# GpSimd waits for landings inside its runs of indirect fetches, in the first sorted mixture of a long graph-network kernel

## The chip, the cores and the metric

The kernel runs on one core of one Trainium2 chip, as one launch. The metric is the device time of one execution in microseconds, the median over runs. Five engines run their own instruction streams beside each other: TensorE (PE), VectorE (DVE), ScalarE (ACT), GpSimd (POOL) and SyncE (SP); they meet only at semaphores and at barriers between blocks.

## The reference

Four graph layers and four feed-forward layers stand in turn, each added to the running x, each fed a layer norm of it. x is 128 graphs of 40 nodes of 128 features, so 5120 rows or 40 tiles of 128 rows. The change lies in the second feed-forward layer (`_L1_ffn_ref`), a mixture of 8 experts of which each row uses its best two:

```python
xn = (x - mu) * rsqrt(var + EPS) * gamma + beta
logits = einsum('bsd,de->bse', xn, Wr) + br
top_vals, top_idx = top_k(logits, 2)
w = softmax(top_vals, axis=-1)
w_full = einsum('bsk,bske->bse', w, one_hot(top_idx, 8))
for e in range(8):
    h = gelu(einsum('bsd,dh->bsh', xn, W1[e]) + b1[e])      # 128 -> 256
    y = y + (einsum('bsh,hd->bsd', h, W2[e]) + b2[e]) * w_full[..., e, None]
x = x + y
```

The third feed-forward layer routes by the result of an attention over a graph of 524288 random edges. Its edges are counted per pair of nodes, and that count is computed ahead, inside the mixture above: it needs nothing of the mixture.

## The kernel before, in words

`sparse_router` (from L1153) sorts the row numbers by expert. Each expert's list is padded to whole tiles of 256 rows (SL, two halves of 128, SLH = 2). There are 47 such tiles (NT). `sparse_moe` (L1671) then runs five streams in one block.

**GpSimd** issues all indirect DMAs, one instruction for 128 rows of 128 floats (64 KB). First 94 fetches (L1710), two for each tile, bring the normalised rows of a tile into one of six buffers `xg` (NX); from the seventh tile on a tile's pair waits until PE has turned the tile six before (`x_ps`). Then it waits until all results are stored in memory (`y_st`), and 80 return fetches (L1724) bring each row's two expert results back. They come in 8 parts (PARTS) of 5 row tiles (CT) with two fetches each. Part n lands on semaphore `c_in[n % 6]`, 16 counts for each fetch. From part 6 on a part first waits for DVE to have used the buffer (`added`).

**PE** turns a tile (L1734), multiplies it by W1 (L1743) and by W2 (L1751), two tiles ahead of the last step. **ACT** moves the turned tile (L1781), applies gelu (L1789) and copies the tile's expert weights into one of three buffers (L1796), which waits for an earlier result. **DVE** adds the bias (L1816), and between tiles does its share of the edge count: `nearest` (L2560: 32 maxima and 32 replacements, L2569) before the first tile, `search` after each. **SP** stores the results (L1855).

After the tiles DVE finishes the search and then works through the 8 parts of the return: for each part 5 or 6 steps `one_hot` (L2604, L2605: bf16 comparisons, 44 in all; PE multiplies each, L2690), then the wait for the part's ten fetches, and then ten multiply-adds into x (L1842). The block ends with DVE's last part; the layer norm of the next block (L351) needs all of it.

The same pattern without the edge count stands in the last layer (`sorted_moe`, results at L1625), and a third run of indirect fetches in `edge_router` (L2988, L2993; DVE's products at L2947). Neither is changed.

The functions that the change touches, as they are before it:

Of the kernel before, what the change touches and what calls it, by code (L numbers as in the profile page):

```python
# [953 lines left out]
SLH = SL // 128  # L954
# [716 lines left out]
def sparse_moe(nc, g, ex, out=None, count=None):  # L1671
# [2 lines left out]
    NX, NY, NW = 6, 4, 3  # L1674
    CT = 5
    PARTS, NC_ = TT // CT, 6
    name = ex.name
    with nc.cleanup_on_exit(), ExitStack() as ctx:
        sb = lambda s, shape: ctx.enter_context(nc.sbuf_tensor(f"{name}_{s}", shape, F32))
# [12 lines left out]
        x_in = [sem(f"x_in{i}") for i in range(NX)]  # L1692
        y_st = [sem(f"y_st{i}") for i in range(NY)]
        c_in = [sem(f"c_in{i}") for i in range(NC_)]
# [4 lines left out]
        @block.gpsimd  # L1699
        def _(pool):  # L1700
            pool.wait_ge(ex.stored, 32)
            if count is not None:
                count.prepare(pool)

            def gather(i):
                if i >= NX:
                    pool.wait_ge(x_ps, i - NX + 1)
                for h in range(SLH):
                    n = SLH * i + h
                    pool.indirect_dma_start(out=xg[:, i % NX, h, :], out_offset=None, in_=ex.xn_dram,  # L1710
                                            in_offset=bass.IndirectOffsetOnAxis(ap=ex.gidx[:, n:n + 1], axis=0)).then_inc(x_in[i % NX], 16)

            for i in range(NT):
                gather(i)
            for b in range(NY):
                pool.wait_ge(y_st[b], stores(b))
            for n in range(PARTS):
                if n >= NC_:
                    pool.wait_ge(added, n - NC_ + 1)
                for t in range(CT):  # L1720
                    if n > 0 and t == CT // 2:
                        pool.wait_ge(c_in[(n - 1) % NC_], 32 * CT * ((n - 1) // NC_ + 1))
                    for c in range(2):
                        pool.indirect_dma_start(out=yc[:, n % NC_, t, c, :], out_offset=None, in_=ex.y_dram,  # L1724
                                                in_offset=bass.IndirectOffsetOnAxis(ap=ex.pidx[:, n * CT + t, c:c + 1], axis=0)).then_inc(c_in[n % NC_], 16)
# [2249 lines left out]
def graph_network(nc, g):  # L3975

    with ExitStack() as ctx:
# [32 lines left out]
        with nc.sbuf_tensor("raw1", [128, TT, D], F32) as raw:  # L4010
            with nc.cleanup_on_exit(), ExitStack() as held:
                affine = (g.L1_ffn_gamma, g.L1_ffn_beta)
                ex = SparseExperts(nc, held, raw[:], g, "f1", 8, g.L1_ffn_W1, g.L1_ffn_b1, g.L1_ffn_W2, g.L1_ffn_b2, True, affine)
                with ExitStack() as early:
                    logits = RawLogits(nc, early, "f1l", 8, g.L1_ffn_Wr, g.L1_ffn_br, ex, affine)
                    raw_norm(nc, g, "n3", logits, twice=True)
                    sparse_router(nc, g, ex, logits)
                sparse_moe(nc, g, ex, count=EdgeCount(nc, held, g, keys, kept.keys_in))
            l2_gnn(nc, g, adjacency, search, tok=raw[:])
# [69 lines left out]
```

## Time and profile before

| | us |
|---|---|
| three runs, median (lowest to highest) | 3129.7 (3127.84 to 3139.87) |
| span of the profiled execution | 3331.1 |
| PE, DVE, ACT, POOL busy in that span | 2524.9, 2094.1, 1309.8, 721.2 |
| first fetch of L1710 to last one | 1658.67 to 1798.62 |
| first return fetch of L1724 to last one | 1823.15 to 1949.29 |
| start of DVE's last group of L1842 | 1993.44 |

The page gives the profiled execution's span and no other time of it; the runs are executions without the profiler. Times of rows are microseconds from the span's start, lengths of single instructions in the groups are ns. "Idle before <-releaser" names what the engine's wait ended with, inferred from semaphore events; "issue" is time in which it waited for nothing that the profile shows. Where a named releaser had long been done, it was another.

### The profile page before, as it was taken

The numbers are of one execution on the slowest core, as the hardware profiler recorded it, in microseconds if no ns is written. First come the engines' busy times: TensorE is split into PE (matmuls) and PEld (weight loads), VectorE is DVE, ScalarE is ACT, GpSimd is POOL, SyncE is SP. The second block draws the span as 40 slices with busy tenths as digits, with TensorE's granted clock in tenths as the row PEclk, the third lists the DMA queues.
The fourth block names the chain that finished last, engine by engine and source line by source line (L and its number), as shares of the span: only waits on it lengthen the run. The fifth ranks groups of instructions, "written<-read, shape, count | busy, mean of one in ns | idle before, by whom it ended". The sixth has DMA issues, their size and how long they took to land. (4 is left out here: it accounts for less than half of the span.)

```text
span 3331.1 us, 50319 instructions
## 1 busy us (share of the span) xinstructions
PE 2524.9 (76%) x18840; PEld 1620.7 (49%) x18840; DVE 2094.1 (63%) x4114; ACT 1309.8 (39%) x2407; POOL 721.2 (22%) x756
## 2 busy tenths in 40 slices
PE   6477999999999999965566178587649989971542
PEld 5334555555555555545255167344326666641542
DVE  6737787778788878856646397654743547761212
ACT  4333444444444444424555004232224444451431
POOL 0000000000000000010064630166610033306244
PEclk7688999999999999987689557698879978885766
DMA  4431112222221121113223101000012221111333
GB/s 76 130 107 42 49 49 49 55 60 53 50 49 49 49 49 49 46 40 121 67 77 75 43 17 18 13 5 5 5 32 70 52 50 41 41 33 56 94 87 93
DMA packets 189058, 178.78 MB, mean 54 GB/s; under 512 B 83700, under 2 KB 162177, under 8 KB 185977
## 3 DMA queue, kind: packets, MB, share of 16 engines
q1 hardware_dynamic: 168064, 137.00, 16.5%
q0 software_dynamic: 20768, 38.75, 4.8%
q8 instruction: 145, 2.38, 0.3%
q14 instruction: 81, 0.66, 0.1%
HBM read 139.11 MB, written 43.64 MB: 55 GB/s over the span
## 5 line engine op out<-in xcount | busy, mean ns | idle before, releaser
L3557 PE MATMUL hy_ps<-hy_uT,hy_win 128*128 128x512 f32 x1152 | 499.3, 594 | 0.0
L3557 PEld LDWEIGHTS hy_ps<-hy_uT,hy_win 128*128 128x128 f32 x1152 | 217.9, 190 | 283.0 <-issue 272.2
L2469 POOL DMA_DIRECT2D ek_w<-ek_src x32 | 17.8, 556 | 1162.6 <-DVE ek_dst L2491 1162.6
L3619 PE MATMUL hy_ps<-hy_wo,hy_yg 128*128 128x512 f32 x512 | 239.6, 613 | 14.5 <-ACT XNP L3762 8.7
L3055 PE MATMUL er_c<-XNG 128*128 128x400 f32 x480 | 184.0, 540 | 0.0
L3619 PEld LDWEIGHTS hy_ps<-hy_wo,hy_yg 128*128 128x128 f32 x512 | 94.2, 193 | 125.6 <-issue 99.3
L2690 PE MATMUL f_px<-XNG 128*128 128x40 bf16 x736 | 69.0, 266 | 98.2 <-DVE XNG L2605 66.0
L3841 DVE TENSOR_TENSOR_SCAN XNG<-XNG,hy_fx 128x2048 f32<-128x2048 f32 x32 | 141.6, 4425 | 3.0 <-issue 0.4
L2988 POOL DMA_INDIRECT er_gone<-er_nodes,er_sidx x120 | 123.7, 1031 | 36.6 <-issue 36.3
L3055 PEld LDWEIGHTS er_c<-XNG 128*128 128x128 f32 x480 | 97.6, 209 | 69.5 <-issue 14.5
L946 DVE TENSOR_TENSOR f_hg<-f_hs,f_gb 128x640 f32<-128x640 f32 x64 | 52.7, 825 | 109.9 <-ACT f_hs L928 91.3
L1625 DVE TENSOR_TENSOR f_ysl<-f_py,f_cur 128x256 f32<-128x256 f32 x54 | 22.9, 424 | 147.3 <-remote 69.4
L2690 PEld LDWEIGHTS f_px<-XNG 128*128 128x128 bf16 x736 | 60.6, 152 | 106.7 <-DVE XNG L2605 74.8
L3692 ACT ACTIVATE hy_swT<-hy_ps 64x160 f32<-64x160 f32 x256 | 76.2, 298 | 83.3 <-PE hy_ps L3524 78.3
L1567 PE MATMUL f_ph<-f_xT,f_cur 128*128 128x256 f32 x216 | 62.2, 414 | 59.6 <-DVE f_xT L1619 35.2
L1548 POOL DMA_INDIRECT XNP<-f_ys,f_pidx x80 | 78.2, 977 | 131.9 <-DMA f_ys<-f_ysl 108.2
L2279 PEld LDWEIGHTS g_ps<-ident,g_P 40*40 40x40 f32 x2048 | 84.3, 129 | 43.6 <-issue 34.1
L2947 DVE TENSOR_TENSOR XNG<-er_VW,er_MD 128x400 f32<-128x400 f32 x112 | 58.4, 573 | 73.4 <-DMA f_y<-f_ysl 54.7
L2252 PE MATMUL g_ps<-g_Z,g_wc 128*128 128x320 f32 x256 | 101.5, 542 | 1.1 <-ACT g_Z L2301 1.1
L1710 POOL DMA_INDIRECT f_xg<-f_xn,f_gidx x94 | 90.3, 961 | 51.0 <-issue 22.9
L1724 POOL DMA_INDIRECT XNP<-f_y,f_pidx x80 | 87.7, 1096 | 63.0 <-issue 23.8
L3792 DVE TENSOR_TENSOR hy_sw<-hy_ps,hy_blg 128x512 f32<-128x512 f32 x64 | 44.3, 692 | 90.7 <-PE hy_ps L3508 90.7
(698 smaller groups left out, 6123.4 us busy)
## 6 DMA issues: line engine op xcount, KB each, us to landing
XNG<-hy_decays SPq DMA_DIRECT2D x32, 1024.0 KB
hy_rb<-hy_inverse SPq DMA_DIRECT2D x128, 128.0 KB, 3.5
f_gb<-gate_rows SPq DMA_DIRECT2D x16, 640.0 KB, 5.1
g_KB<-g_keys SPq DMA_DIRECT2D x32, 320.0 KB
f_xg<-f_rows SPq DMA_DIRECT2D x54, 128.0 KB
f_ys<-f_ysl SPq DMA_DIRECT2D x54, 128.0 KB
f_y<-f_ysl SPq DMA_DIRECT2D x47, 128.0 KB
f_rows<-in_x_dram POOLq DMA_DIRECT2D x2, 2560.0 KB, 16.0
```

The costliest lines, as they stand in the source:

```text
L1548: pool.indirect_dma_start(out=yc[:, n % NC_, t, c, :], out_offset=None, in_=ex.y_dram[n // (PARTS // ex.HALVES)], in_offset=bass.IndirectO ...
L1710: pool.indirect_dma_start(out=xg[:, i % NX, h, :], out_offset=None, in_=ex.xn_dram, in_offset=bass.IndirectOffsetOnAxis(ap=ex.gidx[:, n:n ...
L1724: pool.indirect_dma_start(out=yc[:, n % NC_, t, c, :], out_offset=None, in_=ex.y_dram, in_offset=bass.IndirectOffsetOnAxis(ap=ex.pidx[:, n ...
L2252: mm = pe.matmul(psy, wc[:, h, :], Z[:, c % 2, h].rearrange("p b n -> p (b n)"), start=(h == 0), stop=(h == HD - 1))
L2279: mm = pe.matmul(pst[n % 2][j][rows(j), h, :], P[rows(j), c % 2, h, q, :], g.ident[rows(j), rows(j)], start=True, stop=True)
L2690: mm = pe.matmul(self.ph, self.OL[:, b, :, k], self.OH[:, b, :, k], start=False, stop=False, skip_group_check=True)
L2988: pool.indirect_dma_start(out=gone[:, par, u, :], out_offset=None, in_=tab_dram, in_offset=bass.IndirectOffsetOnAxis(ap=sidx[:, par, u:u + ...
L3055: mm = pe.matmul(flat(acc[j][:]), OD[:, 1 - par, u, j * 128:(j + 1) * 128], flat(X[:, u]), start=False, stop=False, skip_group_check=True)
L3557: mm = pe.matmul(p[:], win[:, t, m * 128:(m + 1) * 128], uT[:, t, :], start=(t == 0), stop=(t == KT - 1))
L3619: mm = pe.matmul(PS[4 + q % 2][:], yg[:, t, q * 128:(q + 1) * 128], wo[:, t, :], start=(t == 0), stop=(t == KT - 1))
L3692: ins = act.activation(o, p[:, :, j, 0:N], ACT.Copy)
L3841: dve.tensor_tensor_scan(L[:, a][:, st], dAb[:, a][:, st], E[:, st], 0.0, ALU.mult, ALU.add)
```

## The change

In `gather(i)` (tiles) GpSimd now waits, before the pair of tile 2 and before that of tile 4, until both fetches of the tile just before have landed. In the return it waits before row tiles 2 and 4 of each part until that part's earlier fetches have landed, and before row tile 0 of parts 1 to 7 until the part before has landed whole. The wait that stood before row tile 2 of parts 1 to 7, for the part before, goes.

```diff
+    BURST = 4
...
             def gather(i):
                 if i >= NX:
                     pool.wait_ge(x_ps, i - NX + 1)
+                elif i > 0 and SLH * i % BURST == 0:
+                    pool.wait_ge(x_in[i - 1], 16 * SLH)
                 for h in range(SLH):
...
                 for t in range(CT):
-                    if n > 0 and t == CT // 2:
+                    if t > 0 and t % (BURST // 2) == 0:
+                        pool.wait_ge(c_in[n % NC_], 32 * (CT * (n // NC_) + t))
+                    elif t == 0 and n > 0:
                         pool.wait_ge(c_in[(n - 1) % NC_], 32 * CT * ((n - 1) // NC_ + 1))
                     for c in range(2):
                         pool.indirect_dma_start(out=yc[:, n % NC_, t, c, :], out_offset=None, in_=ex.y_dram,
```

GpSimd's own order in the tile fetches of the kernel before; an xN stands for N like instructions, and the semaphore names are those of a semaphore's first user (n1_root is `x_ps` here):

```order
L2555 MEMSET ec_zero 128x128
L1710 DMA f_xg<-f_xn,f_gidx 128x128 x12
L1710 DMA f_xg<-f_xn,f_gidx 128x128 [waits n1_root]
L1710 DMA f_xg<-f_xn,f_gidx 128x128
L1710 DMA f_xg<-f_xn,f_gidx 128x128 [waits n1_root]
```

and the same place of the changed kernel (its line numbers are up to 5 higher; hy_ip_ps and hy_dt_half are `x_in[1]` and `x_in[3]`):

```order
L2560 MEMSET ec_zero 128x128
L1713 DMA f_xg<-f_xn,f_gidx 128x128 x4
L1713 DMA f_xg<-f_xn,f_gidx 128x128 [waits hy_ip_ps]
L1713 DMA f_xg<-f_xn,f_gidx 128x128 x3
L1713 DMA f_xg<-f_xn,f_gidx 128x128 [waits hy_dt_half]
L1713 DMA f_xg<-f_xn,f_gidx 128x128 x3
L1713 DMA f_xg<-f_xn,f_gidx 128x128 [waits n1_root]
```

The first twelve fetches are now three groups of four; the rest stands as it did.

The start of GpSimd's return fetches before (the four names at the head are the stores' `y_st`, hy_da_rdy is `c_in[0]`, hy_da_ld `c_in[1]`):

```order
L1724 DMA XNP<-f_y,f_pidx 128x128 [waits hy_dt_rdy,hy_da_exp,hy_dtln,hy_xs]
L1724 DMA XNP<-f_y,f_pidx 128x128 x13
L1724 DMA XNP<-f_y,f_pidx 128x128 [waits hy_da_rdy]
L1724 DMA XNP<-f_y,f_pidx 128x128 x9
L1724 DMA XNP<-f_y,f_pidx 128x128 [waits hy_da_ld]
```

and after the change:

```order
L1729 DMA XNP<-f_y,f_pidx 128x128 [waits hy_dt_rdy,hy_da_exp,hy_dtln,hy_xs]
L1729 DMA XNP<-f_y,f_pidx 128x128 x3
L1729 DMA XNP<-f_y,f_pidx 128x128 [waits hy_da_rdy]
L1729 DMA XNP<-f_y,f_pidx 128x128 x3
L1729 DMA XNP<-f_y,f_pidx 128x128 [waits hy_da_rdy]
L1729 DMA XNP<-f_y,f_pidx 128x128
L1729 DMA XNP<-f_y,f_pidx 128x128 [waits hy_da_rdy]
L1729 DMA XNP<-f_y,f_pidx 128x128 x3
L1729 DMA XNP<-f_y,f_pidx 128x128 [waits hy_da_ld]
```

Where a wait stood behind 14 fetches and then behind every 10, a part of ten is now cut into 4, 4 and 2, and each cut asks for the fetch just sent. On the other engines nothing moves.

## Rows read from the trace of the kernel before

**Rows 1.** Waits of the whole span, three: us in total, times, longest
```profile
DVE f_ysl L1625 <- remote: 69.4, 3, 29.0
...
DVE XNG L2604 <- DMA hy_xn<-XNP: 55.1, 2, 41.1
...
DVE XNG L2947 <- DMA f_y<-f_ysl: 54.7, 5, 11.6
```

**Rows 2.** Table of stretches of this block: length, busy times, clock, DMA
```profile
core 0: us, PE busy (x) PEld busy (x) DVE busy (x) ACT busy (x) POOL busy (x), PEclk, DMA share, GB/s
1666.50:1687.50 21.00, 6.41 (x33) 4.96 (x31) 7.65 (x48) 4.07 (x7) 13.50 (x15) 0.66 0.17 47
...
1847.00:1903.00 56.00, 2.73 (x32) 2.35 (x29) 1.63 (x2) 0.00 (x0) 39.75 (x42) 0.50 0.19 49
1903.00:1996.00 93.00, 64.58 (x689) 56.73 (x689) 89.15 (x166) 0.00 (x0) 29.55 (x20) 0.50 0.06 15
```

**Rows 3.** Instructions in order, return fetches of POOL beside DVE
```profile
1823.15 0.95 POOL L1724 DMA_INDIRECT XNP<-f_y,f_pidx  x1 [23.59 <-DMA f_y<-f_ysl]
...
1860.67 1.22 DVE L2604 TENSOR_TENSOR XNG<-XNG 128x2048 bf16<-128x2048 bf16 x1 [14.01 <-DMA hy_xn<-XNP]
...
1898.29 0.95 POOL L1724 DMA_INDIRECT XNP<-f_y,f_pidx  x1 [0.30 <-issue]
...
1903.37 1.23 DVE L2604 TENSOR_TENSOR XNG<-XNG 128x2048 bf16<-128x2048 bf16 x1 [41.08 <-DMA hy_xn<-XNP]
```

**Rows 4.** Waits of 1657 to 1830 us, this block's tile stage
```profile
DVE work L2569 <- issue: 13.3, 21, 1.3
...
ACT f_xT L1781 <- remote: 12.9, 2, 12.3
```

**Rows 5.** Instructions in order, first tile fetches and who uses them
```profile
1660.05 0.98 POOL L1710 DMA_INDIRECT f_xg<-f_xn,f_gidx  x1 [0.30 <-issue]
...
1662.60 0.95 POOL L1710 DMA_INDIRECT f_xg<-f_xn,f_gidx  x1 [0.30 <-issue]
1662.61 0.69 PE L1734 MATMUL f_px<-ident,f_xg 128*128 128x128 f32 x2 [10.12 <-DMA f_xg<-f_xn,f_gidx]
...
1665.12 0.95 POOL L1710 DMA_INDIRECT f_xg<-f_xn,f_gidx  x1 [0.30 <-issue]
1665.16 0.69 PE L1734 MATMUL f_px<-ident,f_xg 128*128 128x128 f32 x2 [1.86 <-DMA f_xg<-f_xn,f_gidx]
...
1667.72 0.69 PE L1734 MATMUL f_px<-ident,f_xg 128*128 128x128 f32 x2 [0.16 <-issue]
...
1693.33 0.38 PE L1734 MATMUL f_px<-ident,f_xg 128*128 128x128 f32 x2
...
1693.98 0.95 POOL L1710 DMA_INDIRECT f_xg<-f_xn,f_gidx  x1 [4.08 <-PE f_px L1734]
```

**Rows 6.** POOL's return fetches as groups: 1914.8 to 1950.3, then 1823 to 1846.6
```profile
L1724 POOL DMA_INDIRECT XNP<-f_y,f_pidx x20 | 29.5, 1477 | 21.4 <-DVE raw L1842 15.7 <-issue 5.8
...
L1724 POOL DMA_INDIRECT XNP<-f_y,f_pidx x19 | 18.4, 971 | 29.1 <-DMA f_y<-f_ysl 23.6 <-issue 5.5
```

**Rows 7.** Instructions in order, DVE in the return stage
```profile
1916.09 1.22 DVE L2604 TENSOR_TENSOR XNG<-XNG 128x2048 bf16<-128x2048 bf16 x1
...
1919.31 1.22 DVE L2604 TENSOR_TENSOR XNG<-XNG 128x2048 bf16<-128x2048 bf16 x1
...
1924.08 2.88 DVE L1842 SCALAR_TENSOR_TENSOR raw<-XNP,f_gates,raw 128x128 f32<-128x128 f32 x10
...
1926.87 1.22 DVE L2604 TENSOR_TENSOR XNG<-XNG 128x2048 bf16<-128x2048 bf16 x1
...
1993.44 2.87 DVE L1842 SCALAR_TENSOR_TENSOR raw<-XNP,f_gates,raw 128x128 f32<-128x128 f32 x10
```

**Rows 8.** Instructions in order, DVE results once the last tile fetch is sent
```profile
1805.63 0.42 DVE L1816 TENSOR_TENSOR f_ysl<-f_py,f_cur 128x256 f32<-128x256 f32 x1 [0.17 <-PE f_py L1751]
...
1807.60 0.42 DVE L1816 TENSOR_TENSOR f_ysl<-f_py,f_cur 128x256 f32<-128x256 f32 x1 [0.23 <-PE f_py L1751]
```

## The prediction, made before the changed kernel was run

> **What bounds the block now.** I read the block of the change in this order: the table of stretches, the instructions in order for POOL and DVE, the waits, and the groups of POOL's fetches. The reader is to see first that in the profiled execution the block has two holes. From 1666.5 to 1687.5 PE is busy for 6.41 us of 21 and DVE for 7.65, while POOL sends 15 fetches; from 1847 to 1903 DVE is busy for 1.63 us of 56 and POOL sends 42 [rows 2]. In the second hole DVE waits 14.01 and then 41.08 us before a one-hot step, under the name of a DMA of a layer long finished, and goes on 4 us after the last fetch of an unbroken run of 60 was issued (1898.29 + 0.95, against 1903.37) [rows 3]. In the first, ACT waits 12.3 us for a releaser the trace cannot name, and DVE loses 13.3 us in 21 gaps between replacements that wait for nothing [rows 4]. The DMA engines are only 17 to 19% busy there [rows 2], so it is no lack of transfer capacity.
>
> The question that decides the forecast is whether those holes are in the runs as well. The profiled span is 3331.1 us, the median run 3129.7: 201 us more. The same kind of wait, with a releaser that is none, stands in every other block in which POOL sends long runs of fetches: 69.4 us at L1625, 55.1 at L2604, 54.7 at L2947 [rows 1], 179 us in all; with the 13.3 us of rows 4 it is 193. That is nearly the whole difference, and I see no other place in the page for 200 us. I take it that the holes belong to the profiled execution and that the runs have next to none of them. Beside this stands a rule of the Trainium skill (NOTIFIC — the notification-queue block, "Overflow: three behaviours, one of which stalls the engine"): the block that writes the profiler's records holds its producers back rather than lose a record inside. No row here shows such a hold as such. A second rule (SBUF — State Buffer, "SBUF: two separate sides") says that PE and ACT never wait on another engine's port; the trace agrees in so far as the holes stop ACT as well, so a port is not what they are made of.
>
> **The block without the holes.** Two chains then race to the end of the return stage.
>
> DVE: from 1860.67 − 14.01 = 1846.7 [rows 3], where it is done with the search, 44 one-hot steps and 8 groups of adds. Two steps take 1919.31 − 1916.09 = 3.22, so 1.61 each; a group of adds 1926.87 − 1924.08 = 2.79 [rows 7]. 44 × 1.61 + 8 × 2.79 = 93.2 us, which ends at 1939.9.
>
> POOL: its fetches follow each other at 0.971 + 0.30 = 1.27 us where DVE does little, and at 1.477 + 0.30 = 1.77 where DVE is busy without a break [rows 6]: a DVE-busy microsecond costs POOL 0.50 / 1.77 = 0.28. From 1823.15 [rows 3], 80 × 1.27 = 101.6 and 0.28 × 93.2 = 26.3 give 1951.1; 1.6 for the last landing and 2.9 for DVE's last adds give 1955.6. So in the runs POOL, not DVE, ends this stage last, by some 16 us.
>
> **The change part by part.** One wait: PE's transposes of the first three tiles start at 1662.61, 1665.16 and 1667.72, and the second fetch of each tile was generated at 1661.03, 1663.55 and 1666.07 [rows 5], so a landing is known 1.58, 1.61 and 1.65 us later. In place of the gap of 0.30, POOL's next fetch starts after 1.61: a wait adds 1.31 us. No row shows POOL itself waiting for its own fetch. From below, 1.31 less the 0.27 that an engine needs from a release to its start (1693.33 + 0.38 to 1693.98 [rows 5]) is 1.04; from above, with another 0.27, it is 1.58. I take 1.31, the value that the rows give directly.
>
> Return stage: waits before row tiles 2 and 4 of 8 parts, 16, and before row tile 0 of 7 parts, 7: 23 waits, 23 × 1.31 = 30.1 us. Behind each, POOL's queue holds only more fetches, and for those DVE's adds wait. A little comes back: POOL now stands still for 30 of some 158 us, and of DVE's hindrance of 26.3 us that share, 5.0, falls into time in which it generates nothing. Net 25.1: DVE's last adds end at 1980.7 in place of 1955.6. Nothing hides it, since POOL was already last; DVE's 16 us of slack grow.
>
> Tile stage: two waits before fetches 5 and 9, 2.6 us. Here 94 fetches × 1.26 (two in 1665.12 − 1662.60 [rows 5]) = 118 us stand against 47 tiles at 1807.60 − 1805.63 = 1.97 [rows 8] = 93 us for PE, ACT and DVE, so without holes POOL sets this stage too, and 2.6 us reach the end. If DVE's `nearest` still set the pace there, they would be hidden: 0 to 2.6, I take 2.6.
>
> The wait that goes (for the part before, at row tile 2) asked for a fetch sent four earlier, 5 us before, and POOL's gap there is the usual 0.30: it cost nothing and gives nothing.
>
> Sum: 25.1 + 2.6 = 27.7 us on 3129.7, that is 3157, 0.9% more. The ends: without any hindrance by DVE the POOL chain is 1823.15 + 101.6 + 1.6 + 2.9 = 1929.3, DVE's 1939.9 is last before, and 1929.3 + 30.1 = 1959.4 after: +19.5, or 3149. With 1.04 a wait in the main case the sum is 25 × 1.04 − 4 = 22, with 1.58 and nothing absorbed 25 × 1.58 = 39.5, or 3169. So the forecast's own range is 3147 to 3170.
>
> A rule of the Trainium skill gives another size (DMA: Bandwidth & Descriptors, "Anatomy of one DMA — SWDGE (gpsimd) path"): such a DMA takes about 2.0 us plus bytes over 436e3, for 64 KB about 2.15 from start to completion. The trace has 0.98 + 1.58 = 2.56 and decides. By the rule a wait would add 0.9 us and the sum would be about 19, 3149.
>
> **The rivals.**
>
> The holes are real (faster). If the runs stall as the profile does, cutting the runs of fetches into fours takes the holes away, for in the profile holes open only behind long unbroken runs. The tile stage then gives back DVE's 13.3 us [rows 4] less the 2.6. The return stage ends at 1980.7 in place of 1993.44 + 2.87 = 1996.3 [rows 7], 15.6 less. In sum −26.3: 3103. It decides from the point where the holes in the runs are more than some 28 us in this block. For it: the rows themselves, and no row proves what the runs do. Against it: 201 us of difference have then no home. The trace of the changed kernel can look exactly so, with a span shorter than 3331.1, while the runs are longer; this is not a contradiction of the forecast but part of it.
>
> POOL is quicker in the runs (no change). If the 0.30 us between fetches, too, is there only with the profiler, POOL's chain without hindrance is 80 × 0.30 = 24 us shorter, 1905 before and 1935 after, under DVE's 1940. The waits are hidden: 3130. For it: if the profiler costs 200 us elsewhere, it may cost here. Against: the gap is 0.30 everywhere, in holes and out of them, and rows 6 show DVE hindering POOL.
>
> The waits pass at once (no change, 3130). The counts asked for are those of the fetch just sent, whose landing takes 1.6 us, so this has little for it.
>
> **How the numbers follow.** Forecast 0.73, real holes 0.15, quicker POOL 0.10, waits that pass 0.02. A difference under 0.5% (15.6 us, so 3114 to 3145) is what a measurement of this kernel can hardly tell from none. Faster by more: 0.15. Within: 0.12. Slower by more: 0.73. The predicted time is the forecast's, 3157. The range takes in its own 3147 to 3170 with a microsecond above, and reaches down over the cases of no change to 3118, which leaves out the real holes and little more; beside it the forecast's own range is 3147 to 3170.
>
> **What would show it.** In the profile after: about 23 idle times of POOL before return fetches, each about 1.6 us, ended by the DMA of the return; the same twice among the first twelve tile fetches; no wait of 14 or 41 us at DVE's one-hot steps and gaps gone between the first replacements; DVE instead waiting for the return DMA before its adds in the later parts; the other blocks' unnamed waits as before. The forecast is wrong if the runs get faster with the span, or if DVE never waits for the fetches in the later parts.

## The result and the profile after

| | before | after |
|---|---|---|
| runs, median (lowest to highest) | 3134.78 us (3127.84 to 3144.02, 4 runs) | 3179.53 us (3166.32 to 3183.6, 4 runs) |
| ratio of the runs, 95% interval | | 1.0155 [1.012, 1.019] |
| span of the profiled execution | 3331.1 us | 3180.2 us |

The change makes the kernel slower, by 44.8 us. The forecast was slower by 27.7 us, 3157, with a range up to 3171: the direction is right, the size is not, and the range is missed by 8.5 us.

First a correction of what stands above. The profiled executions are not a class beside the runs: each is one of them. That of the changed kernel has a span of 3180.2 us and is the run of 3181.88 us in the list. The 3331.1 us of the first trace of before is an odd execution of that kernel; the longest of its other runs on record took 3152.46 us. So a second trace of the same code (called "before, again" here; its run is the first experiment) is the one to compare with. Its span is 3127.3 us.

The block has two stages: the tile stage, from the first tile fetch to the first return fetch, and the return stage, from there to the end of DVE's last adds. By the table of stretches, first before, again:

```profile
core 0: us, PE busy (x) PEld busy (x) DVE busy (x) ACT busy (x) POOL busy (x), PEclk, DMA share, GB/s
1657.68:1795.08 137.40, 104.70 (x659) 93.01 (x659) 97.47 (x423) 94.33 (x189) 91.05 (x95) 0.92 0.42 91
1795.08:1921.66 126.58, 69.56 (x738) 60.87 (x738) 112.04 (x208) 0.00 (x0) 98.14 (x80) 0.50 0.16 42
```

and after the change:

```profile
1662.93:1803.20 140.27, 105.12 (x659) 92.84 (x659) 97.38 (x423) 94.71 (x189) 90.68 (x94) 0.93 0.41 89
1803.20:1969.68 166.48, 69.46 (x738) 60.77 (x738) 111.75 (x208) 0.00 (x0) 99.05 (x80) 0.50 0.12 32
```

The tile stage grew by 2.9 us, the return stage by 39.9, in sum 42.8. In the return stage DVE and PE are busy for the same time in both, and POOL for 0.9 us more: nothing is done that was not done before, and 39.0 of the 39.9 us are standing still. Neither trace has the holes of [rows 2]: in 1847 to 1903 DVE is busy for 48.47 of 56 us in before, again, and for 33.27 after the change, against 1.63 there.

POOL's fetches as groups, 1640 to 2060 us (the mean is the time in which POOL generates one fetch, its generation), before, again:

```profile
line engine op names shapes xcount | busy us, mean ns | idle before us <-releasers
L1724 POOL DMA_INDIRECT XNP<-f_y,f_pidx x80 | 98.1, 1227 | 42.1 <-issue 24.1 <-DMA f_y<-f_ysl 18.0
```

and after:

```profile
L1729 POOL DMA_INDIRECT XNP<-f_y,f_pidx x80 | 99.0, 1238 | 80.7 <-DMA XNP<-f_y,f_pidx 45.9 <-DMA f_y<-f_ysl 17.8 <-issue 17.1
L1713 POOL DMA_INDIRECT f_xg<-f_xn,f_gidx x94 | 90.7, 965 | 32.2 <-issue 25.7 <-DMA f_xg<-f_xn,f_gidx 4.0 <-PE f_px L1739 2.4
```

This is the group of [rows 6] for the whole stage. There are 23 idle times of 45.9 us in all where gaps of 0.30 stood: 45.9 − 23 × 0.30 = 39.0, so 1.70 us for each wait, against 1.31 in the prediction. The mean generation is 1.238 us against 1.227, 0.9 us over 80 fetches. 39.0 + 0.9 is the 39.9 of the stage.

Instructions in order, POOL after the change. The first two show the usual wait of the return and the third the longest one:

```profile
1809.84 0.96 POOL L1729 DMA_INDIRECT XNP<-f_y,f_pidx  x1 [1.85 <-DMA XNP<-f_y,f_pidx]
1816.40 0.95 POOL L1729 DMA_INDIRECT XNP<-f_y,f_pidx  x1 [1.82 <-DMA XNP<-f_y,f_pidx]
...
1872.62 1.08 POOL L1729 DMA_INDIRECT XNP<-f_y,f_pidx  x1 [3.70 <-DMA XNP<-f_y,f_pidx]
```

In the tile stage, the first of the two waits, PE's transposes released by the same landing, and POOL's next fetch:

```profile
1669.42 0.69 PE L1739 MATMUL f_px<-ident,f_xg 128*128 128x128 f32 x2 [1.71 <-DMA f_xg<-f_xn,f_gidx]
1669.64 0.95 POOL L1713 DMA_INDIRECT f_xg<-f_xn,f_gidx  x1 [1.85 <-DMA f_xg<-f_xn,f_gidx]
1670.90 0.95 POOL L1713 DMA_INDIRECT f_xg<-f_xn,f_gidx  x1 [0.30 <-issue]
```

Eighteen of the 23 idle times lie between 1.74 and 1.92 us; five are longer, 2.13 to 3.70; the median of all is 1.88. The long ones are no scatter: the waits before fetches 19, 35, 61 and 71 of the 80 are above 2.1 us in each of the six traces with these 23 waits, the one before fetch 35 between 2.43 and 3.70. What those fetches have in common no run shows.

The Trainium skill (DMA: Bandwidth & Descriptors, "Anatomy of one DMA — SWDGE (gpsimd) path") fits such a DMA with about 2.0 us plus bytes over 436e3, which makes an estimate of 2.15 us for 64 KB. Here the wait ends 0.95 + 1.85 = 2.80 us after the start of the fetch that it asks for; the trace does not agree, and it decides.

DVE in the return stage, where [rows 7] has the end at 1993.44; before, again:

```profile
1873.31 2.88 DVE L1842 SCALAR_TENSOR_TENSOR raw<-XNP,f_gates,raw 128x128 f32<-128x128 f32 x10 [0.33 <-DMA XNP<-f_y,f_pidx]
1890.28 2.88 DVE L1842 SCALAR_TENSOR_TENSOR raw<-XNP,f_gates,raw 128x128 f32<-128x128 f32 x10 [4.53 <-DMA XNP<-f_y,f_pidx]
1904.47 2.88 DVE L1842 SCALAR_TENSOR_TENSOR raw<-XNP,f_gates,raw 128x128 f32<-128x128 f32 x10 [3.34 <-DMA XNP<-f_y,f_pidx]
1918.78 2.88 DVE L1842 SCALAR_TENSOR_TENSOR raw<-XNP,f_gates,raw 128x128 f32<-128x128 f32 x10 [1.91 <-DMA XNP<-f_y,f_pidx]
```

and after:

```profile
1903.98 2.88 DVE L1847 SCALAR_TENSOR_TENSOR raw<-XNP,f_gates,raw 128x128 f32<-128x128 f32 x10 [9.95 <-DMA XNP<-f_y,f_pidx]
1925.00 2.88 DVE L1847 SCALAR_TENSOR_TENSOR raw<-XNP,f_gates,raw 128x128 f32<-128x128 f32 x10 [8.61 <-DMA XNP<-f_y,f_pidx]
1945.69 2.88 DVE L1847 SCALAR_TENSOR_TENSOR raw<-XNP,f_gates,raw 128x128 f32<-128x128 f32 x10 [9.82 <-DMA XNP<-f_y,f_pidx]
1966.80 2.88 DVE L1847 SCALAR_TENSOR_TENSOR raw<-XNP,f_gates,raw 128x128 f32<-128x128 f32 x10 [8.69 <-DMA XNP<-f_y,f_pidx]
```

In before, again DVE waits for landings before its last four groups of adds, 10.1 us in all, and after the change before its last six, 50.3 us (two lines left out). POOL's chain already ended last; the waits lengthen just that chain.

### The profile page after: what moved, and what is told of

It is laid out like the page before. It is cut to its first block and busy times, and to the rows that moved or that the text cites. A ratio compares the mean times of both kernels' runs of the same rounds, so it can differ in the third digit from the quotient of the medians.

```text
span 3180.2 us, 50321 instructions
## 1 busy us (share of the span) xinstructions
PE 2510.6 (79%) x18840; PEld 1612.8 (51%) x18840; DVE 2094.7 (66%) x4114; ACT 1311.0 (41%) x2407; POOL 730.6 (23%) x756
## 5 line engine op out<-in xcount | busy, mean ns | idle before, releaser
L1729 POOL DMA_INDIRECT XNP<-f_y,f_pidx x80 | 99.0, 1238 | 80.7 <-DMA XNP<-f_y,f_pidx 45.9
L3767 ACT ACTIVATE XNP<-hy_ps,hy_rms 128x512 f32<-128x512 f32 x64 | 42.2, 681 | 148.5 <-PE hy_ps L3624 147.9
L928 ACT ACTIVATE f_hs<-f_ph,f_b1t 128x320 f32<-128x320 f32 x128 | 66.9, 527 | 84.7 <-PE f_ph L896 84.0
L2284 PE MATMUL g_ps<-ident,g_P 40*40 40x40 f32 x2048 | 92.1, 216 | 11.8 <-DVE g_obias L2419 8.1
L3716 ACT ACTIVATE hy_xr<-hy_ps 128x512 f32<-128x512 f32 x80 | 47.8, 598 | 122.8 <-PE hy_ps L3562 122.4
```

What stands on the lines that cost most here:

```text
L928: ins = act.activation(hs[:, e % 2, k, :], psh[e % 2][k][:], ACT.Gelu, bias=b1t[:, e * H2 + k:e * H2 + k + 1])
L2284: mm = pe.matmul(pst[n % 2][j][rows(j), h, :], P[rows(j), c % 2, h, q, :], g.ident[rows(j), rows(j)], start=True, stop=True)
```

## The experiments

Ratios are to runs of the kernel before on the same chip, with 95% intervals. The stages are as above, each from one trace, and differences of a stage are against before, again. The edits are against the kernel before unless said otherwise.

**Before, again** (no edit).

> The kernel before, unchanged, for a second trace of it. The theory that the stalls belong to one disturbed execution and not to the kernel expects a trace with a span near 3135 us, no wait above 5 us at DVE's one-hot steps, and the waits with an impossible releaser in the other two blocks (69, 55 and 55 us in the first trace) gone; the return stage, first fetch to end of DVE's last adds, should then last about 132 us, bound by GpSimd. The rival, that long unbroken runs of fetches always stall the other engines, expects a span near 3330 us and the same holes again.

Ratio 1.0008 [0.9985, 1.0031], span 3127.3 us, tile stage 137.4, return stage 126.6, no hole. None of the three waits of [rows 1] is there: the L1625 wait for an unnamed releaser, 69.4 us there, is gone, and in the tile fetches and the return every gap of POOL is 0.3. The holes belong to one execution.

**The waits before tile fetches alone.**

```diff
+                elif i > 0 and SLH * i % 4 == 0:
+                    pool.wait_ge(x_in[i - 1], 16 * SLH)
```

> Only the two waits before the tile fetches 5 and 9 are added, the return stage is that of before. If GpSimd sets the tile stage, each wait of about 1.7 us beyond the usual gap reaches the end: +3 to +4 us, so 3138 (0.1%). If DVE's work before the first result covers it: 0.

Ratio 0.9993 [0.9968, 1.0017]; tile stage 140.3, 2.9 more, and return stage 124.9. Two idle times make 3.8 us where 0.6 stood: 3.2 us. The runs can't see 3 us, the trace can, and it says that POOL's fetches do set the pace of this stage. The return stage, which has no edit here, is 1.7 us shorter with a mean generation of 1.206 us: two traces of the same return differ by that much.

**The return waits alone**, twice, the second time on the chip of the later experiments.

```diff
-                    if n > 0 and t == CT // 2:
+                    if t > 0 and t % 2 == 0:
+                        pool.wait_ge(c_in[n % NC_], 32 * (CT * (n // NC_) + t))
+                    elif t == 0 and n > 0:
```

> Only the return waits of the change (23 that bite), no tile waits. Theory: nearly all of the loss is here, +40 to +45 us (1.3 to 1.45%). Rival, that the two parts each carry a share: +25 to +30 us here and the rest in the tile stage.

Ratio 1.0105 [1.0074, 1.0136]; tile stage 137.2, return stage 165.9, 39.3 more than before, again. Of POOL's groups:

```profile
L1726 POOL DMA_INDIRECT XNP<-f_y,f_pidx x80 | 100.2, 1252 | 79.0 <-DMA XNP<-f_y,f_pidx 44.3 <-DMA f_y<-f_ysl 17.7 <-issue 17.1
```

The idle times make 44.3 − 6.9 = 37.4 us, the slower generation 2.0. By the stage this is just short of the 40 to 45 us of the theory. The runs show 31 us more, and their interval ends at 1.0136, so for the most part they lie below the 1.3% that it asked for. The rival had 25 to 30 us here and the rest in the tile stage, and that stage has only 2.9 to give.

> The return waits alone again, on the same chip as the whole change: theory (costs add up: the tile waits are worth 2.9 us and the rest scatters): return stage 166, ratio lower than that of the change by 0.001, that is 1.013 to 1.018. Rival (the two parts together cost more than their sum): again 1.010, and the change 1.016 or more, a difference of 15 us or more against the 2.9 of the stage.

Ratio 1.0093 [1.0056, 1.013], return stage again 165.9. The ratio is below the 1.013 of the theory a second time, while the stage is the 166 that it said.

**Only the waits before row tile 0** (7 of the 23).

```diff
-                    if n > 0 and t == CT // 2:
+                    if t == 0 and n > 0:
```

> In the return only the 7 waits before row tile 0 of parts 1 to 7 (for the part before whole), none inside a part, no tile waits. Theory of a fixed price for each wait with GpSimd as the bound: 7 of 23, +12 to +14 us (0.4%). Rival, that GpSimd has slack of some waits before DVE's chain is overtaken: 0 to +5 us.

Ratio 1.0036 [1.0013, 1.0059]; return stage 142.8, 16.2 more:

```profile
L1724 POOL DMA_INDIRECT XNP<-f_y,f_pidx x80 | 102.5, 1282 | 53.3 <-issue 21.9 <-DMA f_y<-f_ysl 17.5 <-DMA XNP<-f_y,f_pidx 13.9
```

Seven idle times cost 13.9 − 2.1 = 11.8 us, 1.69 each, which is the fixed price of the theory. POOL's generation got slower by 0.055 us, 4.4 us in 80, so the stage grew by more than the 12 to 14 us that it expected. Standing still gave nothing back here, and the generation beside DVE got slower.

**The change again**, twice.

> The change itself once more, so that its cost is known better than from four runs. Theory (each of 25 waits costs GpSimd 1.5 to 1.7 us and nothing is given back; by stage the traces gave +39.9 in the return and +2.9 in the tiles): the ratio is 1.0135 (1.012 to 1.015), +42 us. Rival (something outside the block costs a few us more): the ratio stays at 1.0155 or above while the stages by the trace again add to 43. By the prediction's own sum it would be 1.009.

Ratio 1.0196 [1.0168, 1.0224]; stages 140.6 and 165.0, that is +41.6, while the runs are 65 us longer. The theory's 1.012 to 1.015 is missed, and what happened is what the rival had said: 1.0155 or more, with the stages still at about 43.

> The whole change on the same chip as its return waits alone: stages 140.3 and 166.5 us as before, ratio 1.0135 to 1.0195. Theory and rival as for the return waits alone.

Ratio 1.0139 [1.0098, 1.018]; stages 140.0 and 164.2, +40.2. The runs of the change are 12 us above those of the return waits alone on the same chip. The theory had 2.9, the rival 15 or more; both intervals are about 12 us to either side, so the runs decide between neither.

**The same groups of fetches, but POOL waits for the group before the last one.** Each group of 4, 4 and 2 has a semaphore of its own; there are no tile waits, and DVE waits for a part's three semaphores. Of the edit, the waits alone:

```diff
-                    if n > 0 and t == CT // 2:
-                        pool.wait_ge(c_in[(n - 1) % NC_], 32 * CT * ((n - 1) // NC_ + 1))
+                    q = 3 * n + t // 2
+                    if t % 2 == 0 and q >= 2:
+                        p, k = (q - 2) // 3, (q - 2) % 3
+                        pool.wait_ge(c_in[p % NC_][k], (64, 64, 32)[k] * (p // NC_ + 1))
```

> The return fetches stand in the same groups of 4, 4 and 2, but each group has a semaphore of its own and GpSimd waits for the group before the last one, so that up to 8 fetches are under way; 22 waits or so instead of 23, as many semaphore waits in the queue. The waits before tile fetches are not in it. Theory (a wait costs what is left of the landing it asks for, about 2.0 us after the issue; the group asked for was sent at least 2 fetches, 2.5 us, earlier): every gap stays at 0.3, the return stage is 126 to 130 us, ratio 1.000 (0.997 to 1.003). Rival (a wait of GpSimd on a DMA's semaphore has a price of its own, some us, whether or not the landing has come): the stage is 150 to 166 us, ratio 1.008 to 1.012.

Ratio 1.0005 [0.9976, 1.0034], return stage 127.3:

```profile
L1726 POOL DMA_INDIRECT XNP<-f_y,f_pidx x80 | 98.4, 1230 | 41.6 <-issue 23.8 <-DMA f_y<-f_ysl 17.5 <-DMA XNP<-f_y,f_pidx 0.3
```

Twenty-two waits on the same kind of semaphore at the same places cost nothing: the only idle time put down to the DMA is 0.3 us, the usual gap of one fetch. A wait has no price of its own; what costs is asking for the fetch that was just sent.

**Return waits before every row tile** (39), no tile waits. The same edit also went into the return of the last layer's mixture (L1548 before), which the expectation does not say; its return runs by the same code as this one's.

```diff
-                    if n > 0 and t == CT // 2:
+                    if t > 0:
+                        pool.wait_ge(c_in[n % NC_], 32 * (CT * (n // NC_) + t))
+                    elif n > 0:
```

> Return waits before every row tile, 39 instead of 23 (never more than 2 fetches under way); no waits before tile fetches. Theory (1.7 us a wait, in proportion): return stage 126.6 + 39 x 1.7 = 193 us, ratio 1.020 to 1.022. Rival (in shorter bursts a landing is known sooner, since fewer fetches are in front of it: 1.2 us a wait): 173 us, ratio 1.015. Rival (GpSimd recovers from DVE's hindrance while it stands still, as the prediction had it, so that the mean generation falls from 1.25 to about 1.0 us): 193 less some 15 to 20 us.

Ratio 1.0389 [1.0348, 1.0429]; return stage 183.7, 57.1 more:

```profile
L1728 POOL DMA_INDIRECT XNP<-f_y,f_pidx x80 | 92.3, 1153 | 104.8 <-DMA XNP<-f_y,f_pidx 74.8 <-DMA f_y<-f_ysl 17.8 <-issue 12.2
...
POOL XNP L1550 <- DMA XNP<-f_ys,f_pidx: 80.5, 39, 3.1
```

(the second row is from the waits, for the last layer). A wait costs 74.8 / 39 − 0.30 = 1.62 us here, 63 in all, and 5.9 us of generation do come back (1.153 against 1.227). So the 193 of the theory was too much by 9, and the give-back of the rival is a third of what it said. The ratio is far above the 1.022 of the theory because of the second place: in the last layer the time from the first return fetch to the end of the span goes from 112.2 to 177.9 us. 57.1 + 65.7 = 122.8 is what the runs show, 3245.39 − 3123.01 = 122.4.

**DVE's comparisons cut.** All but the first two one-hot steps work on 8 columns instead of the full width, in the kernel before and in the changed one. What this leaves out is the count of the edges, on which a later layer's routing rests; so it is the stages that are compared here. Of the edit, the line that sets the widths:

```diff
+        LO, HI = (self.LO, self.HI) if self.done <= 2 else (8, 8)
```

> The kernel before with all but the first two of DVE's one-hot comparisons on 8 columns instead of the full width, so that DVE has some 55 us less work in the return stage; the count of the edges is not computed by it. Theory (GpSimd ends the return stage last and is slowed only by DVE's busy time): mean generation about 1.0 instead of 1.23 us, return stage 126.6 - 80 x 0.22 = 107 to 112 us, 15 to 20 us less; another 0 to 10 us may come from places outside the stage where the same comparisons stand. Rival (DVE bounds the stage before the change): the stage shrinks by DVE's saving of about 40 to 50 us, to the 105 us of unhindered fetches at least, and DVE's last groups of adds wait for landings where they did not before.

Ratio 0.9962 [0.9944, 0.9979]; return stage 106.2, 20.4 less, with DVE waiting for landings before its last four groups, 2.55 to 4.96 us each. DVE is busy for 57.3 us in the stage instead of 112.0. The 106.2 lies between the 107 to 112 of the theory and the 105 at which the rival's shrinking would stop, so the length alone does not decide. What speaks against the rival is that DVE waited for landings before its last four groups without the cut as well. POOL's group here, and below it that of the changed kernel with the same cut:

```profile
L1724 POOL DMA_INDIRECT XNP<-f_y,f_pidx x80 | 77.5, 969 | 41.6 <-issue 24.1 <-DMA f_y<-f_ysl 17.5
```

> The changed kernel with all but the first two one-hot comparisons on 8 columns (the count of the edges is not computed by it), against the same cut in the kernel before, whose return stage was 106.2 us with a mean generation of 0.969 us. Theory (a wait for a landing costs GpSimd 1.7 us whatever DVE does, since the DMA's own time makes it): return stage 106.2 + 23 x 1.7 = 145, with the mean generation still 0.97. Rival (part of a wait's price is DVE's doing, so a wait costs the predicted 1.31 without it): 136.

```profile
L1729 POOL DMA_INDIRECT XNP<-f_y,f_pidx x80 | 78.7, 984 | 80.0 <-DMA XNP<-f_y,f_pidx 45.4 <-DMA f_y<-f_ysl 17.6 <-issue 17.1
```

Ratio 1.0059 [1.0033, 1.0086]; return stage 145.6. The theory had 145, the rival 136. With the cut the change costs 145.6 − 106.2 = 39.4 us in this stage, without it 39.9: the price of the waits is not the doing of DVE's comparisons.

**A delay without landings.** 28 memsets on POOL before the last part's fetches.

```diff
+    DELAY = 28
...
+                if n == PARTS - 1:
+                    for k in range(DELAY):
+                        pool.memset(xg[:], 0.0).then_inc(idle, 1)
+                        pool.wait_ge(idle, k + 1)
```

> The kernel before, with 28 memsets of the tile buffer (free by then) on GpSimd ahead of the last part's ten fetches, about 1.6 us each with the semaphore between them: a delay of some 45 us in the same block, without any further wait for a landing and without a change in the fetches; DVE stands idle in it. It asks whether the microseconds of the change beyond its two stages (the runs gave +45 to +65, the stages of the traces +42.7) come with any delay here. Theory (time lost here is passed on one to one, and the layers behind only scatter with the clock that they are granted): the stage grows by D as the trace shows it, the ratio is 1 + D/3125, with a margin of 0.002. Rival (a later start of the layers behind costs them clock): the runs grow by 10 to 20 us more than D, and the stretch of the later graph layer shows a lower granted clock.

```profile
L1724 POOL MEMSET f_xg<- 128x1536 f32 x28 | 38.7, 1381 | 1.6
```

The memsets and the gaps between them take 40.3 us, and POOL's generation is 1.7 us shorter than in before, again (96.4 against 98.1), which makes D = 38.6 us. The return stage is 165.2, 38.6 longer, so the delay was passed on whole. Ratio 1.0095 [1.006, 1.0131], that is 30 us with 19 to 41 in the interval. The 1.0124 of the theory is inside that, though the ratio is further from it than the 0.002 it allowed; the 10 to 20 us on top, for a later start of the layers behind, are not there.

**Where the scatter of the runs is.** The stages of the change give +40 to +43 in its three traces, the runs +44.8, +65.0 and +44.8; the return waits alone give +39.3 in the stage, and +31 and +33 in the runs; DVE's cut −20.4 in the stage, and −11 in the runs. The stretch of the later graph layer (L2348 before, from its first instruction on POOL to the next block's), with the return waits alone and in the change again:

```profile
2620.80:2900.40 279.60, 254.48 (x2777) 173.59 (x2774) 202.83 (x230) 150.02 (x326) 101.52 (x33) 0.90 0.15 36
```

```profile
2624.80:2935.70 310.90, 289.78 (x2782) 191.90 (x2780) 203.36 (x230) 150.62 (x329) 101.48 (x32) 0.80 0.13 32
```

DVE, ACT and POOL do the same work in the same time, PE is granted 0.90 of full speed in one and 0.80 in the other (a mix of its two levels, 1.2 and 2.4 GHz), and 31 us lie between. Before, again has 298.1 us at 0.84, the delay 295.8. That stretch alone varies about as much as the runs of a kernel do. In the seven traces of before, again, the change, the return waits alone and the delay, all that follows the block takes 1180.1 to 1215.7 us; they differ by 31.3 us in that stretch and by 8.4 in the rest, 900.5 to 908.9.

The lists of runs give the time and the mean granted clock of each run. Their product counts every microsecond by the clock granted in it, and it hardly scatters: means of 2700 to 2703 us for before (29, 23 and 17 runs), 2722, 2724 and 2726 for the change, 2721 and 2722 for the return waits alone, 2723 for the delay, 2691 for DVE's cut. In the return stage, at a clock of 0.50, 1 us more adds 0.5 to the product. So by an estimate from these means the return waits alone are worth about 2 × 20 = 40 us, the delay also 40, and DVE's cut −2 × 10 = −20, each near its stage. Of the change's 22 some 2.7 come from the tile stage, at its clock of 0.93, and the rest is worth 2 × 19 = 38, some 41 us in all. So most of the difference between the runs and the stages goes with the mean clock. Whether the changed kernel draws a low clock more often than others stays open: in its three traces what follows the block takes 1210.5, 1215.7 and 1213.1 us, in before, again 1205.6, with the return waits alone 1180.1 and 1211.6, with the delay 1200.9.

## Why the prediction was wrong in size

Two steps failed: the price of a wait, 1.31 us where 1.70 was measured, and the 5.0 us that it gave back, of which nothing came. What was right stands first.

**Right: the holes belong to the profiled execution.** Shown by before, again, 204 us shorter in span with the same code. Only the reason was off: it is not that the runs are executions without a profiler, but that this one execution was disturbed. By what, no run shows: none of the 13 other traces repeated it. Of the three waits that were laid to other blocks, the 55.1 us at L2604 are this block's own second hole; the sum of 179 us is not changed by that.

**Right: POOL's chain ends the return stage.** Shown two ways: DVE waits for landings before its last groups in before, again; and a delay on POOL was passed on whole. It fits that with 54.7 us less of DVE's work the stage got shorter by what POOL's generation gained (80 × (1.227 − 0.969) = 20.6 us against 20.4 measured). The stage predicted at 132.5 us measured 126.6. DVE's slack was 10.1 us, not 16.

**Right: the tile stage.** 2.6 us predicted, 2.9 measured, not hidden.

**Wrong: the price of a wait**, the step "a wait adds 1.31 us". It was taken from PE, whose start told when a landing was known. POOL starts later than PE after one and the same landing: fetch 4 of the tiles ends at 1667.79, PE starts at 1669.42, 1.63 us later, and POOL at 1669.64, 1.85 later. In the return a usual idle time is 1.74 to 1.92 us; the median of 1.88 is 1.58 above the usual gap. That is the upper end that the prediction had bounded with an engine's 0.27 us for starting after a release [rows 5], and did not take. Beside these, five of the 23 idle times were longer, four of them at the same fetches in every such trace. They are there with DVE's comparisons cut as well (45.4 us in 23), so the comparisons do not make them; what does is open. In sum the idle times cost 39.0 us in place of 30.1, 8.9 more. In the other two traces of the change a wait cost 1.67 and 1.61 us.

**Wrong: the give-back**, the step "5.0 falls into time in which it generates nothing". The mean generation went up by 0.011 us, so 5.9 us were missing; in the other two traces of the change it was 1.226 and 1.234 us, also no less than before. The instructions in order show where it went. In before, again:

```profile
1842.43 3.29 POOL L1724 DMA_INDIRECT XNP<-f_y,f_pidx  x1 [0.30 <-issue]
...
1876.32 3.77 POOL L1724 DMA_INDIRECT XNP<-f_y,f_pidx  x1 [0.31 <-issue]
```

and after, POOL beside DVE:

```profile
1903.98 2.88 DVE L1847 SCALAR_TENSOR_TENSOR raw<-XNP,f_gates,raw 128x128 f32<-128x128 f32 x10 [9.95 <-DMA XNP<-f_y,f_pidx]
1904.21 0.96 POOL L1729 DMA_INDIRECT XNP<-f_y,f_pidx  x1 [1.87 <-DMA XNP<-f_y,f_pidx]
1905.47 0.95 POOL L1729 DMA_INDIRECT XNP<-f_y,f_pidx  x1 [0.30 <-issue]
1906.73 4.03 POOL L1729 DMA_INDIRECT XNP<-f_y,f_pidx  x1 [0.30 <-issue]
1906.77 1.22 DVE L2609 TENSOR_TENSOR XNG<-XNG 128x2048 bf16<-128x2048 bf16 x1
```

DVE's hindrance is not spread evenly, as the prediction had it. A large part sits in single generations of 3.3 to 4.0 us, over the first one-hot steps behind a group of adds. Before there are four of these, after the change six (3.5 to 4.0; five in each of its other two traces). Beside 0.956 us for an undisturbed generation, all 80 have an excess of 21.7 us before and 22.6 after; these long ones make 9.8 of it before and 16.9 after. The rest did fall, from 11.9 to 5.7, by about what the prediction gave back; the two further long ones and the longer lengths ate it. The wait before row tile 0 asks for the same landing that releases DVE's adds, so both start together (1903.98 and 1904.21) and POOL is generating when the one-hot steps begin. With only those waits the generation is slowest, 1.282 us. That this common start is the cause was read from the traces and not tested by itself.

**The rest.** 8.9 + 5.9 + 0.3 (tile stage) is 15.1: the 27.7 us become 42.8, which the stages show. The measured 44.8 lies 2 us above that, inside the scatter. The measured 3179.5 us is 22 above the forecast's 3157; 5 of these are the kernel before, whose four runs have a median of 3134.8 us where the prediction started from 3129.7. With the terms as measured the forecast would have been 3172.5, still just above its range. And in all three traces of the change together the stages give 41.5 us on average, so that the tenths agree in one trace is partly luck.

**The rivals.** Real holes and a faster kernel: refuted by before, again. A quicker POOL: refuted as far as the traces go, the gap between fetches is 0.30 in all of them. Each of these traces is one of the listed runs, so this holds for the runs. Waits that pass at once: refuted for fetches just sent, and true for the group before the last one. The range was too narrow at the top: its upper end took 1.58 for every wait (25 × 1.58 = 39.5) and no wait longer than the usual one, and nothing at all for the clock of later layers. All but one of the 69 runs of before lie within 17 us of their median, and +65.0 and +44.8 for the same code on one chip show what that does to the median of few runs. Its lower end of 3147 is not worked out there either; the sums give 3149 and more.

## What to carry to other kernels

Here a GpSimd wait for the landing of its own last indirect fetch cost 1.6 to 1.7 us beyond the usual gap, at 23 places one after the other on the chain that ended last. A wait for a group with at least two more fetches (2.5 us) sent behind it cost nothing. To bound how many fetches are under way, ask for the group before the last one. And when one execution's span is far from the list of runs, take a second trace of the same code before reading its waits: here 179 us of three kinds of waits were that execution's own.

## What was not expected of the hardware

- Single indirect-fetch generations on GpSimd of 3.3 to 4.0 us instead of 0.95, each over the first of VectorE's bf16 one-hot steps of 128x2048 behind its adds; with those on 8 columns the mean fell to 0.969 us and none is left.
- More waits do not slow the generation more: 7 waits, at the points where VectorE is released too, raised its mean from 1.227 to 1.282 us, and 39 waits lowered it to 1.153.
- The granted clock of a later stretch with the same work varied between 0.80 and 0.90 from execution to execution, 310.9 against 279.6 us, while what else follows the block stays within 900.5 to 908.9 us in seven traces.
- TensorE starts about 1.6 us after the generation's end of the fetch that it waits for, GpSimd mostly 1.74 to 1.92 us. Where one landing released both, it was 1.63 and 1.85 us, and in the change again 1.56 and 1.77.
- The waits for the landing of the fetch just sent are longer, 2.1 to 3.7 us, before the same four fetches of the return in each of the six traces with 23 of them. The cause is open.
